# Two-layer decoder on one core: gates transposed four batches at once, bias products in separate row groups, and three contexts loaded a stage earlier

## What is computed

```python
router_logits = x @ router_w + router_b
routing_weights = jax.nn.softmax(router_logits, axis=-1)
top_k_weights, top_k_indices = jax.lax.top_k(routing_weights, TOP_K)      # two of eight
...
h1 = jax.nn.gelu(jnp.einsum('btd,nde->btne', x, W1) + b1, approximate=False)
out_per_expert = jnp.einsum('btne,nef->btnf', h1, W2) + b2
output = jnp.sum(out_per_expert * routing_mask[..., None], axis=-2)
```

```python
q = split_heads(query @ Wq.T); k = split_heads(key @ Wk.T); v = split_heads(value @ Wv.T)   # key = value = ctx_1024
q = _apply_rope(q); k = _apply_rope(k)
attn = jax.nn.softmax(jnp.einsum('bhqd,bhkd->bhqk', q, k) * scale, axis=-1)
out = jnp.einsum('bhqk,bhkd->bhqd', attn, v) @ Wo.T + bo
```

## Time and profile before

| | us |
|---|---|
| median of 3 runs | 3318.92 |
| lowest and highest | 3315.80, 3319.88 |
| the profiled execution, its time | 3315.67 |
| its span from first to last instruction | 3313.9 |

### The profile page before, as it was taken

How to read it: one execution, slowest core, us unless ns; L and a number is a source line. 1 busy time by engine, 2 the same in 40 slices (tenths; PEclk the granted TensorE clock), 3 DMA queues, 4 the chain that set the end, 5 groups by cost and what they waited for, 6 DMA issues and landing times. The chain is left out here.

```text
span 3313.9 us, 76444 instructions
## 1 busy us (share of the span) xinstructions
PE 2894.7 (87%) x28264; PEld 2058.5 (62%) x28264; DVE 2309.9 (70%) x5010; ACT 1675.5 (51%) x3320; POOL 956.0 (29%) x1222
## 2 busy tenths in 40 slices
PE   7998999999999996858996999999987989846881
PEld 6886566666665664647884566666656777734660
DVE  5997566677676774457885666666655999965666
ACT  4775555555555553334553344444435777733440
POOL 0000344555555554330001000000001244445551
PEclk9998999999999997789998999999998999968995
DMA  7920444555455552360001333333314777755558
GB/s 172 292 81 4 135 139 127 157 159 149 139 140 155 159 150 71 108 187 15 0 0 40 68 68 69 68 65 68 68 37 132 218 219 227 228 181 148 160 154 238
DMA packets 364744, 413.73 MB, mean 125 GB/s; under 512 B 107993, under 2 KB 330465, under 8 KB 364321
## 3 DMA queue, kind: packets, MB, share of 16 engines
q1 hardware_dynamic: 218128, 220.60, 25.5%
q10 hardware_dynamic: 127216, 139.94, 15.3%
q0 software_dynamic: 19104, 49.22, 4.5%
HBM read 125.30 MB, written 252.45 MB: 114 GB/s over the span
## 5 line engine op out<-in xcount | busy, mean ns | idle before, releaser
L2160 DVE TENSOR_REDUCE x_top<-x_scores 112x2 f32<-112x750 f32 x256 | 231.2, 935 | 120.9 <-PE x_scores L2017 116.4
L1364 ACT ACTIVATE x_probs<-x_held,x_minus_top 112x488 f32<-112x488 f32 x256 | 177.5, 694 | 261.0 <-DVE x_minus_top L1420 261.0
L1414 DVE SCALAR_TENSOR_TENSOR x_held<-x_scores,x_keep 112x976 f32<-112x976 f32 x128 | 150.3, 1174 | 173.7 <-PE x_scores L1291 161.1
L809 POOL TENSOR_TENSOR x_rstd<-x_var,g_minus_half 112x1 f32<-112x1 f32 x128 | 74.6, 583 | 681.8 <-DVE x_var L805 681.2
L1237 POOL TENSOR_TENSOR x_probs<-x_probs,x_inverse 112x488 f32<-112x488 f32 x256 | 250.4, 998 | 10.2
L1278 PE MATMUL x_ring<-w_xkv,x_kv 128*122 128x512 f32 x512 | 236.9, 595 | 0.4 <-ACT x_k L927 0.4
L1271 PE MATMUL x_ring<-x_kv,w_xkv 128*128 128x488 f32 x512 | 232.5, 587 | 1.1 <-ACT x_kv L1340 1.1
L2126 ACT ACTIVATE x_probsT<-x_scores 125x1792 f32<-125x1792 f32 x96 | 159.8, 1664 | 79.6 <-PE x_scores L2036 79.6
L2017 PE MATMUL x_scores<-x_slots 32*112 32x375 f32 x1024 | 170.8, 537 | 29.3 <-DVE x_top L2160 14.2
L809 POOL TENSOR_TENSOR a_rstd<-a_var,g_minus_half 112x1 f32<-112x1 f32 x64 | 35.6, 555 | 539.4 <-DVE a_var L805 539.4
L1232 POOL TENSOR_TENSOR x_inverse<-x_sums,x_minus_one 112x2 f32<-112x2 f32 x128 | 89.6, 700 | 298.7 <-ACT x_probs L1364 298.7
(11 more groups left out here) (482 smaller groups left out, 7537.7 us busy)
## 6 DMA issues: line engine op xcount, KB each, us to landing
expert_slots<-d_empty ACTq DMA_DIRECT2D x32, 3612.0 KB, 17.7
by_position<-r_by_position SPq DMA_DIRECT2D x64, 784.0 KB
first_slots<-d_empty SPq DMA_DIRECT2D x8, 3612.0 KB, 34.4
r_bias<-by_position SPq DMA_DIRECT2D x64, 392.0 KB
m_rows<-expert_slots SPq DMA_DIRECT2D x143, 129.0 KB
x_kq_swapped<-x_kq_raw ACTq DMA_DIRECT2D x64, 243.5 KB
x_slots<-x_kq SPq DMA_DIRECT2D x512, 30.4 KB
m_rows<-expert_replies SPq DMA_DIRECT2D x32, 448.0 KB, 9.5
```

The source lines that it names most:

```text
L1364: nc.scalar.activation(self.probs[u % 6][0:T, :], self.held[m % 2][0:T, i, :], ACT.Exp, scale=self.scale, bias=self.minus_top[0:T, m % 2, ...
L1414: nc.vector.scalar_tensor_tensor(self.held[m % 2][0:T, :, :], self.scores[0:T, 1024 * (m % 2):1024 * (m % 2 + 1)].rearrange("t (i c) -> t ...
L2160: nc.vector.tensor_reduce(self.top[0:T, g, 2 * half:2 * half + 2], self.scores[0:T, 1024 * half:1024 * (half + 1)].rearrange("t (a c) -> t ...
```

## The change

In the first experts POOL zeroes a tile `spread` (128 x 32 batches x 32), and DVE copies the gates of all batches into it, eight columns of every 32. One transpose then turns four batches at once into 128 rows, so that batch i of a group lies in rows 32i to 32i + 7. Eight transposes are made where there were 32, into two banks, and ACT makes two copies where there were eight. `b2` is loaded four times, to rows 0, 32, 64 and 96. The two matmuls of a half now read different row groups and write different banks (`biases`: banks 4 and 5, or 6 and 7). ACT's copies for the last four batches go two before and two behind the gates' copies; DVE's copy of `b1` goes behind the bias; `turn(0)` waits for the last add. In Context attention the three context buffers belong to a stack around both stages, whose semaphore has its own release; SP fills them in the Rotary stage, one after another, and its first load in Context attention is the fourth. POOL fills set 0 of the tiles in frame 1, set 1 in frame 2, set 2 in frame 3, each behind that frame's norm step.

```diff
@@ -327,8 +327,11 @@
                     run_attention(nc, G, CausalAttention, W)
                     run_attention(nc, G, LatentAttention, W)
                     first_experts(nc, G, M, W1, ahead)
-            run_attention(nc, G, RotaryAttention, W1)
-            run_attention(nc, G, ContextAttention, W1)
+            with ExitStack() as both:
+                sb, _, sem = allocators(both, "c1")
+                G["contexts"], G["context_loaded"] = [sb(f"context{i}", [P, CC, D]) for i in range(3)], sem("context_loaded")
+                run_attention(nc, G, RotaryAttention, W1)
+                run_attention(nc, G, ContextAttention, W1)
             G["S2"] = allocators(layer1, "l1")[0]("stream2", [P, NB, D])
             G["dispatch"] = Dispatch(nc, G, layer1, W1)
             run_attention(nc, G, RelativeAttention, W1)
...
         for dst, src in late["loads"]:
             sp.dma_start(dst, src).then_inc(late["loaded"], 16)
+        for b, context in enumerate(self.G["contexts"]):
+            at_least(sp, self.G["context_loaded"], 16 * b)
+            sp.dma_start(context[0:CK, :, :], self.G["t"]["ctx_1024"][b].rearrange("(c p) d -> p c d", p=CK)).then_inc(
+                self.G["context_loaded"], 16)
         sp.wait_ge(late["loaded"], 16 * len(late["loads"]))
...
-        self.ctx = [sb(f"ctx{i}", [P, CC, D]) for i in range(N)]
+        self.ctx = self.G["contexts"]
...
             N = self.plan.turns
-            if not isinstance(e, int) or e + 1 < NB:
+            if not isinstance(e, int) or N <= e + 1 < NB:
                 self.ready(sp, "ctx0", e)
                 load(e + 1, (par + 1) % N)
             if not isinstance(e, int) or 0 <= e - 1 < NB:
                 place(e - 1, (par - 1) % N)
-        load(0, 0)
         frames(sp, NB - 1, body, ahead=self.plan.ahead - 1, behind=self.plan.behind + 1,
                turns=self.plan.turns, unroll=self.plan.unroll)
...
-    def set_up_tiles(self, pool):
+    def set_up_tiles(self, i):
         gp = self.nc.gpsimd
-        for i in range(self.plan.turns):
-            gp.tensor_copy(self.slots[i][:, :, 0:S2], bc(bc(self.const("row16"), 1, HG)[:, :, 0], 2, S2)).then_inc(self.set_up, 1)
-            gp.memset(self.slots[i][:, :, S2:KQ], 0.0).then_inc(self.set_up, 1)
-            gp.memset(self.v[i][:], 1.0).then_inc(self.set_up, 1)
-        gp.memset(self.top_wide[:], 0.0).then_inc(self.set_up, 1)
+        gp.tensor_copy(self.slots[i][:, :, 0:S2], bc(bc(self.const("row16"), 1, HG)[:, :, 0], 2, S2)).then_inc(self.set_up, 1)
+        gp.memset(self.slots[i][:, :, S2:KQ], 0.0).then_inc(self.set_up, 1)
+        gp.memset(self.v[i][:], 1.0).then_inc(self.set_up, 1)
+        if i == 0:
+            gp.memset(self.top_wide[:], 0.0).then_inc(self.set_up, 1)
+
+    def tiles_set_up(self, eng, b):
+        if isinstance(b, int) and b < self.plan.turns:
+            eng.wait_ge(self.set_up, 3 * (b + 1) + 1)
 
     def pool(self, pool, name, b, par, chain):
         if name == "stats":
             self.norm_power(pool, self.norm, b)
-            if isinstance(b, int) and b == 0:
-                self.set_up_tiles(pool)
+            if isinstance(b, int) and 1 <= b <= self.plan.turns:
+                self.set_up_tiles(b - 1)
         elif name == "rope":
             pool.wait_ge(self.turned, b + 1)
-            if isinstance(b, int) and b == 0:
-                pool.wait_ge(self.set_up, 3 * self.plan.turns + 1)
+            self.tiles_set_up(pool, b)
...
-    b2 = W1["pT"][:].rearrange("p c r -> p (c r)")[0:E0, 0:D]
+    b2 = W1["pT"][:].rearrange("p c r -> p (c r)")[:, 0:D]
...
-             (M["rb"][:], t["L0_ffn_router_b"].partition_broadcast(P)), (b2, t["L0_ffn_b2"]),
-             (M["b1"][:], t["b1T"])]
+             (M["rb"][:], t["L0_ffn_router_b"].partition_broadcast(P)), (M["b1"][:], t["b1T"])]
+    loads += [(b2[SLOT * i:SLOT * i + E0, :], t["L0_ffn_b2"]) for i in range(4)]
...
-        gatesT = [sb(f"gatesT{i}", [P, Q * T]) for i in range(2)]
+        spread = sb("spread", [P, NB, SLOT])
+        gatesT = sb("gatesT", [P, NB // Q, T])
...
-        bank = [psum(f"bank{i}") for i in range(8)]
+        four = psum("four", (P, 4 * 512))
+        bank = [psum(f"bank{i}") for i in range(4)] + [four[:, 512 * i:512 * (i + 1)] for i in range(4)]
+        biases = [four[0:T, 1024 * i:1024 * (i + 1)].rearrange("t (q c) -> t q c", c=512)[:, :, 0:D] for i in range(2)]
...
         @block.gpsimd
         def _(pool):
+            pool.memset(spread[:, :, :], 0.0).then_inc(gates_zeroed, 1)
...
         @block.tensor
         def _(pe):
-            def gates_to_rows(g):
-                at_least(pe, gates_ready, g - 1)
+            def gates_to_rows(half):
                 for i in range(Q):
-                    ins = nc.tensor.transpose(bank[4 + g % 2][0:E, i * T:(i + 1) * T], there.gates[0:T, g * Q + i, :],
+                    g = Q * half + i
+                    ins = nc.tensor.transpose(bank[half][:, i * T:(i + 1) * T], spread[0:T, g * Q:(g + 1) * Q, :].rearrange("t q e -> t (q e)"),
                                               const("ident", T)[:, 0:T])
                 ins.then_inc(gates_turned, 1)
 
             def bias(g):
-                pe.wait_ge(gates_ready, g + 1)
+                pe.wait_ge(gates_ready, g // Q + 1)
                 for h in range(2):
-                    at_least(pe, bias_added, 2 * (g - 1) + h + 1)
-                    for i in (2 * h, 2 * h + 1):
-                        ins = nc.tensor.matmul(bank[6 + h][0:T, (i - 2 * h) * D:(i - 2 * h + 1) * D], gatesT[g % 2][0:E, i * T:(i + 1) * T],
-                                               b2, start=True, stop=True)
+                    at_least(pe, bias_added, 2 * g + h - 1)
+                    for i in range(2):
+                        group = slice(SLOT * (2 * h + i), SLOT * (2 * h + i) + E)
+                        ins = nc.tensor.matmul(biases[h][:, i, :], gatesT[group, g, :], b2[group, :], start=True, stop=True)
                     ins.then_inc(bias_ready, 1)
 
             nc.tensor.matmul(bank[2][0:E, 0:1], there.held[(LAST + 1) % 2][0:T, 0, :], ones[0:T, 0:1], start=True, stop=True).then_inc(counted, 1)
+            pe.wait_ge(gates_spread, 1)
             gates_to_rows(0)
             gates_to_rows(1)
             bias(0)
+            bias(1)
             pe.wait_ge(tiled, 1)
             nc.tensor.matmul(bank[3][0:E, 0:1], part("upto0", E), tiles, start=True, stop=True).then_inc(ended, 1)
-            gates_to_rows(2)
-            bias(1)
+            bias(2)
             pe.wait_ge(listed, 1)
             nc.tensor.matmul(bank[2][0:1, 0:PADDED0], ones[0:E, 0:1], passed, start=True, stop=True).then_inc(placed, 1)
             nc.tensor.matmul(bank[3][0:1, 0:PADDED0], weight, passed, start=True, stop=True).then_inc(placed, 1)
-            for g in range(2, NB // Q):
-                if g + 1 < NB // Q:
-                    gates_to_rows(g + 1)
+            for g in range(3, NB // Q):
                 bias(g)
...
-            pe.wait_ge(gates_ready, NB // Q)
+            pe.wait_ge(bias_added, NB // 2)
             turn(0)
             turn(1)
-            pe.wait_ge(bias_added, NB // 2)
...
-            def gates_rows(g):
-                act.wait_ge(gates_turned, g + 1)
-                at_least(act, bias_ready, 2 * (g - 1))
-                nc.scalar.activation(gatesT[g % 2][0:E, :], bank[4 + g % 2][0:E, 0:Q * T], ACT.Copy).then_inc(gates_ready, 1)
-
-            for i in range(Q):
+            def gates_rows(half):
+                act.wait_ge(gates_turned, half + 1)
+                nc.scalar.activation(gatesT[:, Q * half:Q * (half + 1), :].rearrange("p g t -> p (g t)"), bank[half][:, 0:Q * T],
+                                     ACT.Copy).then_inc(gates_ready, 1)
+
+            def room(i):
                 nc.scalar.activation(final[0:T, K * i:K * (i + 1), 0:D], bc(there.xn[LAST % 2 * 4 + i][0:T, :], 1, K),
                                      ACT.Copy).then_inc(copied, 1)
-            for g in range(NB // Q):
-                gates_rows(g)
+
+            room(0)
+            room(1)
+            gates_rows(0)
+            gates_rows(1)
+            room(2)
+            room(3)
...
-            chain.link(nc.vector.tensor_copy(weights[:, :, 2 * D], M["b1"][:, :]))
...
+            dve.wait_ge(gates_zeroed, 1)
+            nc.vector.tensor_copy(spread[0:T, :, 0:E], there.gates[0:T, :, :]).then_inc(gates_spread, 1)
...
             add_bias(0)
+            add_bias(1)
...
-            add_bias(1)
+            add_bias(2)
             dve.wait_ge(placed, 2)
...
-            for g in range(2, NB // Q):
+            for g in range(3, NB // Q):
                 add_bias(g)
+            chain.link(nc.vector.tensor_copy(weights[:, :, 2 * D], M["b1"][:, :]))
             dve.wait_ge(tabled, 2)
```

17 lines of the change are left out of this document (7 added, 10 removed).

## The result

The changed kernel takes 3295.33 us, the median of three runs (3292.39 to 3296.89), against 3318.92 before: 23.6 us less, ratio 0.9924, 95% interval 0.9904 to 0.9944. The prediction said 3295.5 in a range of 3289.0 to 3305.0, and faster by over 0.2% with a chance of 0.93. The interval of the ratio is 6.6 us either way, so the time alone bears out the size of the gain only roughly. The profiled execution took 3292.39 us, its span is 3290.4.

A forecast was written before the change was run, and what follows sets the result against it. TensorE's bias passes bound first experts' start; Context attention's start lacked TensorE work, later frames were TensorE-bound. Gains 18.0 + 5.4 = 23.4 us off 3315.67 gave 3292.3, plus 3.25 to the median: 3295.5 us, range 3289 to 3305.

The forecast's parts named there:

- Head of first experts: Start of first experts: zeroing 0.9, gates' copy 0.3, transposes 1.7 us, so first bias matmul at 1319.9, 0.2 us later.
- Pace: Bias halves in first experts: two row groups overlap, the round trip through two buffers sets 0.99 us a half.
- Last add: End of the bias adds in first experts: 1336.7, with 0.3 us for the table's small steps 1337.0, instead of 1355.3.
- Entry of the loop: First experts' tile loop: first tile copy 1.0 us behind the last add instead of 0.72, an allowance of 0.3 us.
- Context attention: Start of that stage: TensorE starts 5.4 us sooner, plus 0.4, gain 5.8 us; 5.4 net of the added release.
- The chain to the rotation keeps its length: Context attention's fill: the path to the rotation stays as long, or up to 1.3 us shorter if the clock holds.
- frame 3's 3.93 us of cover: Context attention: VectorE's wait for TensorE behind the norm step, 3 to 4 us of it used up by POOL's fills.
- The release: End of Context attention: the contexts' stack adds a release with its barrier, costing 0.4 us.
- No overlap at K = 8: Rival, first experts' bias matmuls: row groups don't overlap, total gain only 11.8 us, time 3307.1; chance 0.07.
- Fills that hold VectorE up: Rival, Context attention frames 1 to 3: POOL's moved fills delay VectorE, up to 12 us back, 3307.5; chance 0.10.
- Late tiles: Rival, start of first experts' tile loop: tiles or scatters land late, for example 4 us lost, 3299.5; chance 0.03.
- A clock that stays down: Rival, Context attention: TensorE longer at 1.2 GHz, up to 20 us more a frame, two give 3335.5; chance 0.03.

## Why the prediction was right, and where it was not

**Head of first experts.** 2.9 us forecast from the stage's first instruction to the first bias matmul, 2.98 measured in the experiments too (1318.95 - 1315.97). Right, with one thing unseen: the small step ahead of the gates' copy took 0.81 us beside POOL's zeroing (0.16 before), and the copy of the gates came behind both.

**Pace.** 0.99 us a half forecast from the pair of row groups in the scores, 1.035 measured (2.07 us a group). The reason given, round trip and not TensorE, was shown from both sides: 1.7 us without overlap, 0.67 with a third pair. The rule of the Trainium skill weighed there ("TensorEngine Tiling (Array Packing)", Theoretical Speedup) gives up to four times for so few rows; the factor measured at K = 8 is 2.7: four matmuls in four row groups took 1.21 us for their eight passes, 0.15 each, against 0.41 in one group. The pace that the prediction drew from it, the adds' own, came only with the third pair of banks: what a single engine could do wasn't the bound.

**Last add.** Forecast 1337.0, 20.0 us into the stage; measured 20.1 in four kernels, 22.5 in the profile of the result, where a stall of unknown origin stood. From 38.3 to 20.1: 18.2 us, against 18.3.

**Entry of the loop.** The term that was mis-sized: 0.3 us allowed, 0.85 measured (1.57 behind the last add against 0.72). The prediction allowed for `turn(0)` behind the last add and for `b1`'s copy; it had not seen that the loop's load of registers stands behind that copy. VectorE was idle there for 1.02 us, where before it was 0.31. Net gain of this half up to the loop: 18.2 - 0.85 = 17.3 us, for 18.0. The loop kept its length (74.4 us in the kernel with contexts alone, 73.7 to 74.5 in the four with this half as it is), and the tiles were not late.

**Context attention.** 5.8 us less 0.4 forecast. The contexts came in time, their loads cost Rotary nothing (283.0 to 284.3 us with them in the experiments, 284.5 without), TensorE started 5.2 us sooner against the stage's first instruction, the norm step took 0.41 us alone. Two steps of the reasoning failed in opposite directions. "The chain to the rotation keeps its length" did not hold: the first rotation gained 4.4 us, 0.8 less than TensorE's start. TensorE's clock was 0.50 for all of the first 6.0 us after its first matmul, where before it stood at 0.86 in the stretch from 4.0 to 6.0 us, so `k0` took 2.84 us instead of 2.56 and `q` 1.67 instead of 1.04. That stretch before, and `q` before and after:

```profile
1788.30:1790.30 2.00, 2.00 (x12) 1.46 (x12) 0.00 (x0) 0.62 (x2) 2.00 (x4) 0.86 0.34 121
```

```profile
1789.08 1.04 PE L912 MATMUL x_ring<-x_xT,w_cq 128*128 128x112 f32 x8
```

```profile
1766.54 1.67 PE L915 MATMUL x_ring<-x_xT,w_cq 128*128 128x112 f32 x8
```

And the steady frames gained more than the first: 5.1 to 6.8 us at the sixth rotation in the six kernels with this half as it is, 6.0 in the profile of the result. The gain still stands at the twelfth rotation (243.2 us into the stage before, 236.4 to 238.0 now); the whole stages vary by more behind it, 735.0 and 737.9 us with the old half and 727.4 to 731.8 with the new one. Most of what comes on top comes in the fourth frame, 21.0 us at a clock of 0.92 where the kernel before took 22.5 at 0.85; the third had lost 0.6. With the fills in frame 0 the gain grows from 0.6 to 2.3 us in the same way, so it goes with the earlier start and not with the moved fills. Why the clock came back sooner there wasn't tried and stays open. The moved fills held up one step each (3.62, 3.15 and 3.15 us for 0.41) and not the one behind it, and used 2.2 us of frame 3's 3.93 us of cover, not 3 to 4. The release cost 0.23 us (idle 1.30 in place of 1.07 at the change to Relative attention), not 0.4. Net 4.9 to 6.6, for 5.4.

**Sum.** 17.3 + 4.9 to 6.6 are 22.2 to 23.9 us, for 23.4; the medians differ by 23.6 and 23.3. The first profile's parts (14.2 and 4.3) were too small in part for reasons outside the change, the waits for "remote", and its other stages were too short for reasons outside it as well; that these cancelled, and that the median came within 0.2 us of the forecast where single runs differ by 4.5, is luck. What bears the forecast out are the instructions' places in the eight profiles of the experiments.

**Rivals.** No overlap at K = 8: out, and its price, 11.6 us, measured as 11.4. Fills that hold VectorE up: the holding-up is real, and no wait that set the path was for it. Late tiles: not here; they appear only when the loop starts 5 us sooner still. A clock that stays down: of the prediction's signs of being wrong, this one came in part, since the fill had more time at 0.50; it cost 0.8 us there, and nothing for whole frames.
